# Passage between the two halves of a two-stage kernel: constants of the second half loaded earlier, the last rows' gamma and beta on another engine

## The reference

```python
f = fftshift(fft2(x)); amp, phase = abs(f), angle(f)
mod = amp * sigmoid(amp @ w_h + b_h) + amp * sigmoid(amp @ w_l + b_l)
spatial = real(ifft2(ifftshift(mod * exp(1j * phase))))
y = silu(conv3x3(spatial, w_f) + b_f) + x
z1 = (y - mean(y)) * rsqrt(var(y) + 1e-3) * gamma + beta      # over channels
```

```python
u = layernorm(z1) * ln1_w + ln1_b
y = mamba2(u, in_proj, conv_w, dt_bias, A_log, D, ssm_norm_w, out_proj)   # state-space scan
z = z1 + weight_norm_linear(y, ff_g, ff_v, ff_b)
out = z + fc2(gelu(fc1(layernorm(z) * ln2_w + ln2_b)))     # fc1, fc2 weight-normed
```

## Time and profile before

| | us |
|---|---|
| median of 3 runs | 4249.27 |
| lowest, highest | 4245.84, 4251.49 |
| the profiled execution: its time | 4248.45 |
| the profiled execution: its span | 4246.5 |

### The profile page before, as it was taken

How to read it: one execution, slowest core, us unless ns; L and a number is a source line. 1 busy time by engine, 2 the same in 40 slices (tenths; PEclk the granted TensorE clock), 3 DMA queues, 4 the chain that set the end, 5 groups by cost and what they waited for, 6 DMA issues and landing times.

```text
span 4246.5 us, 94479 instructions
## 1 busy us (share of the span) xinstructions
PE 3975.6 (94%) x31687; PEld 2858.3 (67%) x31687; DVE 3487.8 (82%) x8772; ACT 3152.6 (74%) x4936; POOL 2582.5 (61%) x2713
## 2 busy tenths in 40 slices
PE   7998899899989994899999999999999999999998
PEld 4787578758875883566666666666666666666665
DVE  4568557754876384899999999999999999999997
ACT  4445534553555253899999999999999999999997
POOL 0036104600560065688888888888888888888886
PEclk9999999999999997999999999999999999999999
DMA  2013101400240022111111111111111111111110
GB/s 91 1 53 129 58 9 61 161 11 12 73 157 0 14 85 77 36 40 40 42 40 42 40 37 42 40 42 40 40 39 40 42 40 42 40 37 42 40 42 26
DMA packets 214857, 205.85 MB, mean 48 GB/s; under 512 B 14368, under 2 KB 149152, under 8 KB 214688
## 3 DMA queue, kind: packets, MB, share of 16 engines
q1 hardware_dynamic: 214688, 203.60, 14.8%
HBM read 136.45 MB, written 67.11 MB: 48 GB/s over the span
## 4 chain that ended last, share of the span: by engine, by line
PE 59%; ACT 0%; DVE 0%; POOL 0%; issue 0%; POOLq 0%; DVEq 0%; ACTq 0%
PE g_ps L1084 7%; PE g_ps L1069 6%; PE g_ps L1027 6%; PE g_ps L1013 5%; PE g_ps L1072 5%; PE g_ps L1101 5%; PE g_ps L1044 3%; PE g_ps L1114 3%; PE g_ps L1120 3%; PE g_ps L1093 3%; PE g_ps L1053 3%; PE g_ps L1018 3%; PE g_ps L1033 2%; PE g_ps L1109 2%; PE g_ps L1006 2%; PE g_ps L1038 1%
## 5 line engine op out<-in xcount | busy, mean ns | idle before, releaser
L1396 DVE TENSOR_TENSOR g_mmat<-g_emat,g_ps 128x1024 f32<-128x1024 f32 x512 | 598.9, 1210 | 1.3 <-PE g_ps L1044 1.3
L1235 ACT ACTIVATE g_emat<-g_ps 128x1024 f32<-128x1024 f32 x512 | 521.3, 1025 | 86.3 <-PE g_ps L1072 84.8
L1339 DVE SCALAR_TENSOR_TENSOR g_acc<-g_ps,g_conv_w,g_acc 128x504 f32<-128x504 f32 (+1 forms) x768 | 554.5, 722 | 10.9 <-ACT g_acc L1198 9.2
L914 POOL TENSOR_TENSOR g_acc<-g_acc,g_tap 128x508 f32<-128x508 f32 x384 | 482.2, 1270 | 126.1 <-DVE g_acc L1339 126.1
L654 POOL MEMSET f_s_hi<- 128x192 f32 x4 | 1.0, 258 | 761.0 <-PE f_ps L345 761.0
L1084 PEld LDWEIGHTS g_ps<-g_mmat,g_dtx 128*32 128x32 f32 x8192 | 192.8, 109 | 310.4 <-issue 213.4
L1069 PE MATMUL g_ps<-g_rz,g_l 128*128 128x512 f32 x1024 | 391.3, 463 | 1.6 <-DVE g_z L1424 1.6
L229 PE MATMUL f_ps<-f_s_hi,f_wf_hi 128*128 128x256 f32 x1152 | 360.6, 313 | 4.9 <-DVE f_s_lo L489 4.9
L1084 PE MATMUL g_ps<-g_mmat,g_dtx 128*32 128x128 f32 x8192 | 329.3, 279 | 0.0
L230 PE MATMUL f_ps<-f_s_lo,f_wf_hi 128*128 128x256 f32 x1152 | 326.6, 284 | 0.0
L424 ACT ACTIVATE f_s_hi<-f_ps 128x384 fp32r<-128x384 f32 x256 | 125.6, 491 | 270.5 <-PE f_ps L217 265.2
(11 more groups left out here) (193 smaller groups left out, 12319.1 us busy)
## 6 DMA issues: line engine op xcount, KB each, us to landing
f_xt<-in_x_cols SPq DMA_DIRECT2D x32, 1024.0 KB, 10.9
f_xres<-in_x SPq DMA_DIRECT2D x128, 256.0 KB, 2.8
z<-f_zout SPq DMA_DIRECT2D x128, 256.0 KB, 2.0
g_zin<-z SPq DMA_DIRECT2D x128, 256.0 KB, 2.6
g_zres<-z SPq DMA_DIRECT2D x128, 256.0 KB, 2.9
out<-g_outb SPq DMA_DIRECT2D x128, 256.0 KB, 2.9
f_wf_raw<-in_w_f SPq DMA_DIRECT2D x1, 576.0 KB, 7.1
g_wx<-in_in_proj_t SPq DMA_DIRECT2D x1, 192.0 KB, 2.4
```

The lines of the kernel that those rows point to most:

```text
L914: pool.tensor_tensor(acc[:, j, :, 1:], acc[:, j, :, 1:], tap1[:, j, :, 0:P - 1], ALU.add).then_inc(add_p[j], 1)
L1235: act.activation(emat[:, g, :].rearrange("p (b n) -> p b n", b=2), ps[:, D_BANK[g]:D_BANK[g] + 2, :], ACT.Exp).then_inc(e_a[g], 1)
L1339: dve.scalar_tensor_tensor(out=acc[:, j, :, k:], in0=four(ps[:, bank, :])[:, :, 0:P - k], scalar=conv_w[:, j, 3 - k:4 - k], in1=acc[:, j, ...
L1396: dve.tensor_tensor(mmat[:, g, :].rearrange("p (h n) -> p h n", h=HEADS), emat[:, g, :].rearrange("p (h n) -> p h n", h=HEADS), ps[:, CB, ...
```

## The change

Three things are changed.

1. The tiles of the sequence half's constants get a class of their own, `StepConstants`, that places them at the start address, ahead of all other tiles of that half (they were mixed with them before). Their 28 loads are no longer at the start of the second block: SP issues them in the last image, seven behind each of the loads of residual 28 to 31. SP waits for the image's last `s_mm` first, in all four images now (three before). The semaphore `win` lives around both blocks.
2. In the last image gamma and beta of parts 28 to 31 are done by VectorE, behind its last moments, with two new semaphores, `f_gamma_tail` and `f_z_tail`. GpSimd, whose last image is now written out, leaves the four parts out, and SP's last four stores wait for VectorE.
3. VectorE no longer waits for `const_a` ahead of the first quad.

```diff
+        self.loads = [(self.ident[:, :], a["ident"]), (self.tri[:, :], a["tri"]), ...
@@ spectral_block, SP
-                if not last:
-                    seen = sp.snap(b * UNITS + UNITS)
-                    sp.wait_ge(s_mm, seen)
-                    sp.sem_inc(waited)
+                seen = sp.snap(b * UNITS + UNITS)
+                sp.wait_ge(s_mm, seen)
+                sp.sem_inc(waited)
                 for j in range(4):
                     xres_load(j + 28, j)
                     if not last:
                         for t in range(2):
                             x_tile(b + 1, 2 * j + t)
+                    else:
+                        for dst, src in const.loads[j::4]:
+                            sp.dma_start(dst, src).then_inc(win, 16)
                     z_store(j + 24, j)
                 for j in range(4):
-                    z_store(j + 28, j)
+                    if last:
+                        sp.wait_ge(z_tail, j + 1)
+                        sp.dma_start(four_columns(sp, z1, b, j + 28), zout[:, j, :]).then_inc(z_out[j], 16)
+                    else:
+                        z_store(j + 28, j)
@@ spectral_block, VectorE, behind the last moments
+                else:
+                    for n in range(4):
+                        z = zout[:, n, :].rearrange("p (r c) -> p r c", r=4)
+                        dve.wait_ge(ln_done, b * PARTS + (n + 29))
+                        dve.tensor_tensor(z, z, gamma[:, :].unsqueeze(1).to_broadcast([P, 4, C]), ALU.mult).then_inc(gamma_tail, 1)
+                        dve.wait_ge(gamma_tail, n + 1)
+                        dve.tensor_tensor(z, z, beta[:, :].unsqueeze(1).to_broadcast([P, 4, C]), ALU.add).then_inc(z_tail, 1)
@@ spectral_block, GpSimd
-                    if k >= 3:
+                    if k >= 3 and not (last and k - 3 >= BATCHES - 2):
                         for h in range(2):
                             affine(k - 3, h)
+            with pool.Fori(0, IMAGES - 1) as b:
+                image(b, False)
+            image(IMAGES - 1, True)
@@ sequence_block
-        sb = Place(nc, "g_")
+        sb = Place(nc, "g_", const.end)
-            for dst, src in loads:
-                sp.dma_start(dst, src).then_inc(win, 16)
@@ sequence_block, VectorE
             dve.wait_ge(const_d, 3)
-            dve.wait_ge(const_a, 2)
```

More of the change, by code:

```diff
@@ L56, in four_columns, with __init__, col @@
     return t[ds(sp.snap(b), 1), :, ds(sp.snap(j * 4), 4), :].rearrange("o h w c -> (o h) (w c)")
-def spectral_block(nc, a, z1):
+class StepConstants:
+    def __init__(self, nc, a):
+        sb = Place(nc, "g_")
+        self.ident, self.tri = sb("ident", [P, P]), sb("tri", [P, P])
+        self.wx, self.wz, self.wdt = sb("wx", [P, 3 * P]), sb("wz", [P, 2 * P]), sb("wdt", [P, HEADS])
+        self.conv_w, self.conv_b = sb("conv_w", [P, 3, 4]), sb("conv_b", [P, 3])
+        self.lncol, self.fc1_b, self.dcol = sb("lncol", [P, 4]), sb("fc1_b", [P, 1]), sb("dcol", [P, 2])
+        self.dtb, self.alog = sb("dtb", [P, HEADS]), sb("alog", [P, HEADS])
+        self.ssm_w, self.op_raw = sb("ssm_w", [P, 2]), sb("op_raw", [P, DINNER])
+        self.vraw, self.gcol = sb("vraw", [P, 3, P]), sb("gcol", [P, 3])
+        self.ffb, self.fc2b = sb("ffb", [P, P]), sb("fc2b", [P, P])
+        self.ind_h, self.ind_g, self.negm = sb("ind_h", [P, HEADS]), sb("ind_g", [P, 4]), sb("negm", [P, 1])
+        self.end = sb.at
+        def col(src):
+            return src.rearrange("(p o) -> p o", o=1)
+        self.loads = [(self.ident[:, :], a["ident"]), (self.tri[:, :], a["tri"]), (self.wx[:, :], a["in_proj_t"][:, 256:640]),
+                 (self.wz[:, :], a["in_proj_t"][:, 0:256]), (self.wdt[:, :], a["in_proj_t"][:, 640:648]),
+                 (self.conv_w[:, :, :], a["conv_w"].rearrange("(j p) k -> p j k", j=3)), (self.conv_b[:, :], a["conv_b3"]),
+                 (self.dcol[:, :], a["d_cols"]), (self.ssm_w[:, :], a["ssm_w2"]),
+                 (self.lncol[:, 0:1], col(a["ln1_w"])), (self.lncol[:, 1:2], col(a["ln1_b"])),
+                 (self.lncol[:, 2:3], col(a["ln2_w"])), (self.lncol[:, 3:4], col(a["ln2_b"])), (self.fc1_b[:, :], col(a["fc1_b"])),
+                 (self.dtb[:, :], a["dt_bias"].partition_broadcast(P)), (self.alog[:, :], a["A_log"].partition_broadcast(P)),
+                 (self.op_raw[:, :], a["out_proj_w"]), (self.vraw[:, 0, :], a["ff_v"]), (self.vraw[:, 1, :], a["fc1_v"]),
+                 (self.vraw[:, 2, :], a["fc2_v"]), (self.gcol[:, 0:1], col(a["ff_g"])), (self.gcol[:, 1:2], col(a["fc1_g"])),
+                 (self.gcol[:, 2:3], col(a["fc2_g"])), (self.ffb[:, :], a["ff_b"].partition_broadcast(P)),
+                 (self.fc2b[:, :], a["fc2_b"].partition_broadcast(P)), (self.ind_h[:, :], a["ind_h"]),
+                 (self.ind_g[:, :], a["ind_g"]), (self.negm[:, :], a["negm"])]
@@ L60, in spectral_block @@
+def spectral_block(nc, a, z1, const, win):
     ctx = ExitStack()
@@ L133, in spectral_block @@
         y_done = sems("f_y_done", 2)
+        gamma_tail, z_tail = sem("f_gamma_tail"), sem("f_z_tail")
         xres_in, z_out = sems("f_xres_in", 4), sems("f_z_out", 4)
@@ L648, in _, with image @@
             pool.wait_ge(mhalf_ready, 1)
-            with pool.Fori(0, IMAGES) as b:
+            def image(b, last):
                 pool.wait_ge(t_mm, b * 32 + 32)
@@ L757, in four, with sequence_block @@
     return t.rearrange("p (g n) -> p g n", g=4)
-def sequence_block(nc, a, z1, out):
+def sequence_block(nc, a, z1, out, const, win):
     ctx = ExitStack()
@@ L769, in sequence_block @@
         HD = 4 * HEADS
-        sb = Place(nc, "g_")
-        ident, tri = sb("ident", [P, P]), sb("tri", [P, P])
-        ident_b, mask_b = sb("ident_b", [P, P], BF), sb("mask_b", [P, P], BF)
[L774 to L781, removed]
+        sb = Place(nc, "g_", const.end)
+        ident, tri, wx, wz, wdt = const.ident, const.tri, const.wx, const.wz, const.wdt
+        conv_w, conv_b, lncol, fc1_b, dcol = const.conv_w, const.conv_b, const.lncol, const.fc1_b, const.dcol
+        dtb, alog, ssm_w, op_raw = const.dtb, const.alog, const.ssm_w, const.op_raw
+        vraw, gcol, ffb, fc2b = const.vraw, const.gcol, const.ffb, const.fc2b
+        ind_h, ind_g, negm = const.ind_h, const.ind_g, const.negm
+        ident_b, mask_b = sb("ident_b", [P, P], BF), sb("mask_b", [P, P], BF)
+        aexp, vsq = sb("aexp", [P, HEADS]), sb("vsq", [P, 3])
         vn, wt = sb("vn", [P, 3, P]), sb("wt", [P, 3, P])
         wc = sb("wc", [P, 2, P])
-        ffb, fc2b = sb("ffb", [P, P]), sb("fc2b", [P, P])
         mhalf, ones = sb("mhalf", [P, 4]), sb("ones", [P, P])
-        ind_h, ind_g, negm = sb("ind_h", [P, HEADS]), sb("ind_g", [P, 4]), sb("negm", [P, 1])
         zin, zres, outb = (sb(n, [P, 2, 4, P]) for n in ("zin", "zres", "outb"))
@@ L844, in sequence_block @@
         add_p, sqs_p = sems("add_p", 3), sems("sqs_p", 2)
[L846 to L860, removed]
+        loads = const.loads
         NLOADS = 16 * len(loads)
@@ L1544 @@
     out = nc.dram_tensor("out", (QUADS, W, 4 * C), FP, kind="ExternalOutput").ap()
-    spectral_block(nc, a, z1)
-    sequence_block(nc, a, z1, out)
+    const = StepConstants(nc, a)
+    with nc.semaphore("g_win") as win:
+        spectral_block(nc, a, z1, const, win)
+        sequence_block(nc, a, z1, out, const, win)
     r = _run(nc, [arrays], core_ids=[0])
```

1 line of the change is left out of this document (removed).

## The result

| | before | changed |
|---|---|---|
| median, us | 4248.35 (4 runs, 4245.84 to 4251.49) | 4221.47 (4 runs, 4220.87 to 4223.48) |
| ratio, 95% interval | | 0.9937, 0.992 to 0.9954 |
| span of the profiled execution | 4246.5 | 4219.1 |

The changed kernel is 26.9 us faster where 26.1 was forecast, and lies inside the range. All nine runs of the changed kernel have a median of 4223.5, the runs of before, 39 over four comparisons, one of 4249.3.

What follows compares the result with a forecast made beforehand. The sequence half is bound by TensorE, so only the passage between the halves can move: 6.9 - 0.15 + 19.3 = 26.05, say 26.1 us saved, 4249.27 - 26.1 = 4223.2 us; range 4216 to 4231.

Steps and rivals of the forecast that it cites:

- The passage: Where the halves meet, from the first half's tail to the first quad's turn on TensorE; all saved there reaches the end.
- The tail: End of the first half: earlier last root, gamma and beta on VectorE, last store at 1659.1 for 1666.07, 6.9 us saved.
- the row of batch 13: Profile row of GpSimd's root beside a busy VectorE: 2.93 us, taken for the last root; 2.42 alone.
- the rule of one wait for the gamma of part 28: Cross-check on the last root: it starts behind one 0.69 us VectorE gamma and ends at 1654.5.
- The constants in SP's queue: 28 loads, seven at a time, in the last image: residual 31 not delayed, 2 us of slack, cost zero.
- The rival: The constants delay residual 31: at 1.3 us an issue, 3.8 us lost, 4227.0 us; chance 0.05.
- Between the blocks: From the last store's release to the second block, 8.87 us: two more clears cost at most 0.2 us, taken as 0.15.
- The start: Second block's start to TensorE's first turn: T + 10.1 for T + 29.43, 19.3 us saved, bounds 17.8 to 19.5.
- TensorE's clock: First quads of the second half: zero taken; rival that it comes up otherwise, 4218.8 or 4232.0 us, chance 0.05.
- The tail was shortened: Answers the rival that something other than the last store holds the barrier: 4230.1 us; tail or start together 0.05.
- the 15 us of waiting: Rival at the second half's start: something hidden there takes half of 14.1 us back, 4230.3; tail or start together 0.05.
- the slower rival: New tile addresses slow the sequence loop, paid 128 times: at 0.3 us a quad, 4261.6 us; chance 0.03.

Runs made afterwards that it cites:

- the second comparison: The changed kernel, unedited, run again beside the kernel before on the same chip: 4227.17 us against 4249.92, ratio 0.995 (0.9936 to 0.9963).

## Why the prediction was right

**What bounds it.** Right. The passage is the place that the change acts on, and the loop takes nothing of its 25.5 us back: from the write of `g_outb` of one quad to the next, it is 19.60 us in both kernels (116 of them take 2273.13 us before and 2273.50 changed). Where the pipeline drains, up to 1.8 us may be lost to the change (above); that was no term of the sum.

**The tail.** Right mechanism, 6.35 us for 6.9. The root starts 0.19 us behind the moments (I had put none), and takes 3.34 for 2.93: the row of batch 13 was the nearest one, but there VectorE ran a mix of shorter instructions, and beside 512-wide products the root is slowed by 0.8 to 0.9, not 0.5 (the term that was mis-sized most). The other way, by the rule of one wait for the gamma of part 28, was short for the same reason: GpSimd's second instruction was held as well, by the beta. ScalarE and VectorE behind it took what I had put.

**The constants in SP's queue.** Zero, as taken; the slack was 1.6 us for 2. The rival is real: an issue more in each group delays store 25 and store 26, so by the slack of 1.6 us and twice 0.47 us an issue it would begin at nine in a row (an estimate; seven and fourteen were run).

**Between the blocks.** 0.42 for 0.15. The two clears cost 0.12; the 0.30 I had not seen, and it came back in the next stage.

**The start.** 19.58 for 19.3, by the steps that I had named: table, chain, statistics at T + 4.31 (4.7), `zin` not late, the turn at T + 9.85 (10.1), held by the last constant tile, with GpSimd's operand ready within 0.4 us of it. The 0.3 that I was off by is the 0.30 of GpSimd's: with its images in one loop the turn comes at T + 10.17.

**TensorE's clock.** I took zero between -4.4 and +8.8. My reason, that the same work in the same order meets the same clock, doesn't hold: the same program differs by 4.2 us in the first quads from one execution to the next. Whether the mean over executions is zero, these runs don't show. The profiled executions happened to differ by 1.9 us in the clock's favour (-2.94 and +1.05), which is why the spans differ by 27.4 and the passage by 25.5. The closeness of 4223.2 to 4221.47 is partly luck (the second comparison put the gain at 22.8 us); the closeness of 26.05 to 25.5 isn't.

**The other rivals.** The tail was shortened, so the barrier hangs on the last store. Nothing was hidden behind the 15 us of waiting. The new addresses cost next to nothing: the same 116 quads took 2273.13 us at the old ones and 2273.35 to 2273.64 at the new ones in 13 traces, 0.2 to 0.5 us, where the slower rival needed 26.

## What to carry to other kernels

Between two phases of a kernel count every engine's way from its last work to its first, since each microsecond there goes to the end whole, however small a share of the page it is: loads that the second phase waits for at its start belong in idle places of the first phase's queues, with a check of what stands behind them (here seven issues in a row were free and fourteen cost 6.3 us). Semaphores cleared one by one between blocks are work like any other, 0.07 us each. And where the gain is a few microseconds of 4200, compare the stages around the edit, which here repeat to 0.1 us, and not the totals, which spread by 12 for the changed kernel alone.

## What the runs showed that I had not expected

- The granted clock of TensorE behind a pause is not the same from execution to execution of one program: from the first turn to the first output 53.0 to 57.7 us in 14 traces, with the clock up within the first 8 us, or at the lower level for those 8 us and its mean below full for up to 24 more.
- Two 0.69 us products on VectorE with both inputs in SBUF stretch GpSimd's 0.24 us instructions on 8 elements per partition to 0.64 and 0.75 us. The 1.66 us power that began ahead of the next such product was not stretched; the one that began behind it took 2.06.
- Writing GpSimd's last image out behind its loop moves 0.30 us from behind the next block's start to ahead of it, and changes A to C by 0.04.
